# A four-layer graph network on one core: rows spread over the partitions by transfers, the projection a round ahead, a new order of steps

## What is computed

```
x = layernorm(x + L0(x, adj))    # s1, s2 = Wh @ a1, Wh @ a2
                                 # att = softmax(leaky_relu(s1[i] + s2[j]), masked by adj);  att @ Wh
x = layernorm(x + L1(x, adj))    # softmax of leaky_relu(bilinear logits), elu(x W1 + att x W2)
x = layernorm(x + L2(x, adj))    # 4-head attention, softmax over j; relu(heads @ Wo + bo)
x = layernorm(x + L3(x, adj))    # relational convolution; adj is 0 or 1, so one relation is live
```

## Time and profile before

| | |
|---|---|
| time, median of 3 runs | 496.18 us (496.12 to 496.77) |
| profiled execution | 496.9 us |
| its span, first to last instruction | 495.0 us |
| busy TensorE / ScalarE / VectorE / GpSimd | 468.4 / 428.0 / 410.8 / 370.6 us |
| mean granted TensorE clock | 0.988 |

### The profile page before, as it was taken

The page is one execution under the profiler, slowest core; times in us unless marked ns, Lnnn a source line. Parts: engine busy times, 40 slices in busy tenths (PEclk is TensorE's granted clock), DMA queues, the critical chain, the costliest instruction groups (busy, mean ns, idle before and its releaser), DMA issues. The chain is left out here.

```text
span 495.0 us, 13988 instructions
## 1 busy us (share of the span) xinstructions
PE 468.4 (95%) x3872; PEld 402.3 (81%) x3872; DVE 410.8 (83%) x1605; ACT 428.0 (86%) x1261; POOL 370.6 (75%) x736
## 2 busy tenths in 40 slices
PE   6968999999999999999999999999999999999793
PEld 5756778988888888988888888888888888877572
DVE  5657898998888998898888988898898989876653
ACT  3558999999999999999999999999999999988750
POOL 1365576788888888888888888888888888986523
PEclk9989999999999999999999999999999999999997
DMA  7211111122112221222112221221123100000011
...
DMA packets 40222, 26.93 MB, mean 54 GB/s; under 512 B 2641, under 2 KB 39889, under 8 KB 40146
## 3 DMA queue, kind: packets, MB, share of 16 engines
...
...
## 5 line engine op out<-in xcount | busy, mean ns | idle before, releaser
L1211 POOL TENSOR_SCALAR x<-y,minus_mean,rstd 128x128 f32<-128x128 f32 x244 | 144.8, 601 | 6.8 <-issue 5.1
L788 ACT ACTIVATE p<-p,nmax 128x256 f32<-128x256 f32 x256 | 128.5, 530 | 0.4 <-DVE nmax L981 0.4
L981 DVE CUSTOM_DVE_ANT_0 p<-ps,neg 128x256 f32<-128x256 f32 x256 | 90.7, 420 | 2.3 <-PE ps L564 2.3
L1193 POOL TENSOR_TENSOR rstd<-ve,minus_half 128x2 f32<-128x2 f32 x128 | 91.1, 712 | 0.0
L575 PE MATMUL ps<-ident,p 128*128 128x128 f32 x512 | 78.0, 275 | 4.1 <-DVE nmax L981 3.4
L1186 POOL TENSOR_SCALAR ve<-stats 128x2 f32<-128x2 f32 x128 | 24.6, 192 | 72.3 <-DVE stats L896 64.9
L797 ACT COPY p2T<-ps 128x512 f32<-128x512 f32 x128 | 75.2, 590 | 1.3 <-PE ps L575 0.5
L575 PEld LDWEIGHTS ps<-ident,p 128*128 128x128 f32 x512 | 61.3, 143 | 9.3 <-DVE nmax L981 4.0
L788 ACT ACTIVATION_READ_ACCUMULATOR p<-p,nmax 128x1 f32 x256 | 56.1, 219 | 0.0
L896 DVE BATCH_NORM_STATS2 stats<-y 128x6 f32<-128x256 f32 x128 | 54.1, 423 | 1.5
L1175 POOL TENSOR_TENSOR relu<-relu,neg 128x512 f32<-128x512 f32 x32 | 37.1, 1161 | 21.1 <-ACT relu L757 21.1
(11 more groups left out here) (130 smaller groups left out, 1210.3 us busy)
## 6 DMA issues: line engine op xcount, KB each, us to landing
...
```

The source lines that it names most:

```text
L788: last = nc.scalar.activation(p2(n)[:, k, a, :], p2(n)[:, k, a, :], ACT.Exp, bias=nmax2(n)[:, k, a:a + 1], scale=-1.0, accum_out=sum2(n)[: ...
L981: last = nc.vector.tensor_tensor_reduce(p2(n)[:, k, a, :], bank("sc2", n, a)[:, k * N:(k + 1) * N], neg2(n)[:, k, :], -1.0, HIGHEST, ALU.a ...
L1193: nc.gpsimd.tensor_tensor(rstd[layer](n), ve[layer](n), minus_half[:, :], ALU.pow)\
L1211: last = nc.gpsimd.tensor_scalar(dst[:, k, 0:D], y_t[layer](n)[:, k, :], minus_mean[layer](n)[:, k:k + 1], rstd[layer](n)[:, k:k + 1], ALU ...
```

## The change

**s2 by transfer.** From graph 3 on, s2_rows and c_s2 do not run. The projection gets a column more (131), so that xw0 has s2 and 0.2 s2 side by side. s2_out stores these two columns to DRAM (256 pieces of 8 bytes), s2_in loads them back as one row of 512 numbers into all 128 partitions (256 KB), the two values of a node next to each other. e0 then takes both inputs from SBUF, each at every second word. xw0 gets 4 buffers for 3, s2row 3 for 2.

**Reciprocal rows by transfer.** rs_rep is gone. rs_rows transposes the 128 x 8 reciprocals once, c_rs copies 8 x 128 to rs_turned, and rs_in spreads each of the 8 rows over 32 partitions by two transfers from SBUF to SBUF. onT2 waits for these.

**Signals.** The two signals of a layer's variance and mean become one counted twice.

**Order.** All places are new. The projection runs one round earlier against sc2, pT0 one round earlier, hg3 one round later, store one round later; the three flag steps stand at the end; the weights are loaded ahead of the second xT and the first adj.

```
-    "sync": [("ld_xT", 6707), ("ld_adj", 7906), ("ld_w", 8043), ("ld_x", 8602), ("aside", 16291), ("store", 19013)],
+    "sync": [("ld_xT", 7696), ("ld_w", 7941), ("s2_out", 8199), ("s2_in", 9000), ("ld_adj", 9574), ("ld_x", 10290),
+        ("rs_in", 14953), ("aside", 16550), ("store", 20067)],
...
+PE_ROWS = 3
...
+    **{step: (0, PE_ROWS) for step in ("s2_rows", "c_s2")},
+    **{step: (PE_ROWS, 0) for step in ("s2_out", "s2_in")},
...
+            def rs_in(n):
+                sp.wait_ge(sem("rs_sb"), n + 1)
+                free(sp, "rs_row", n, "onT_sb")
+                for k in range(T):
+                    sp.dma_start(rs_row(n)[:, k * P:(k + 1) * P],
+                                 rs_turned(n)[k * HEADS:(k + 1) * HEADS].rearrange("h (a i) -> h a i", a=1)
+                                 .broadcast_to((HEADS, DK, P))).then_inc(sem(f"rs_in{n % RING['rs_row']}"), 16)
+
+            def s2_out(n):
+                sp.wait_ge(sem("wh_sb"), n + 1)
+                sp.dma_start(s2_dram[n].rearrange("(t p) c -> p t c", p=P), xw0(n)[:, :, 1:3])\
+                    .then_inc(sem(f"s2_out{n % 2}"), 16)
+
+            def s2_in(n):
+                sp.wait_ge(sem(f"s2_out{n % 2}"), 16 * ((n - PE_ROWS) // 2) + 16)
+                free(sp, "s2row", n, "e0_ready")
+                sp.dma_start(s2row(n).rearrange("p j c -> p (j c)"),
+                             s2_dram[n].rearrange("(a j) c -> a (j c)", a=1).broadcast_to((P, 2 * N)))\
+                    .then_inc(sem(f"s2_in{n % RING['s2row']}"), 16)
...
             def rs_rows(n):
...
-                pe.wait_ge(sem("rs_rep_ready"), n + 1)
-                for k in range(T):
-                    last = pe.transpose(o[:, k * P:(k + 1) * P], rs_rep(n)[:, k, :], ident[:, :])
-                last.then_inc(sem("rs_ps"), 1)
+                pe.wait_ge(sem("rsum2_ready"), n + 1)
+                pe.transpose(o[0:T * HEADS, 0:P], rsum2(n).rearrange("p t h -> p (t h)"), ident[:, :])\
+                    .then_inc(sem("rs_ps"), 1)
...
             def e0(n):
-                dve.wait_ge(sem("s2_sb"), n + 1)
+                if n < PE_ROWS:
+                    dve.wait_ge(sem("s2_sb"), n + 1)
+                    row = bank("s2_rows", n)[:, 0:N]
+                else:
+                    dve.wait_ge(sem(f"s2_in{n % RING['s2row']}"), 16 * ((n - PE_ROWS) // RING["s2row"]) + 16)
+                    row = s2row(n)[:, :, 0]
                 free(dve, "p0", n, "pT_ps0")
                 for k in range(T):
...
+                    last = nc.vector.scalar_tensor_tensor(out=p0(n)[:, k, :], in0=row, scalar=xw0(n)[:, k, 0:1],
+                                                          in1=s2row(n)[:, :, 1], op0=ALU.add, op1=ALU.max)
...
-            def rs_rep_(n):
-                pool.wait_ge(sem("rsum2_ready"), n + 1)
-                free(pool, "rs_row", n, "rs_ps")
-                nc.gpsimd.tensor_copy(rs_rep(n).rearrange("p t (h d) -> p (t h) d", h=HEADS),
```

More of the change, by code:

```diff
@@ L191, in build @@
         eq1 = ring("eq1", [T, N])
-        xw0_all = sb("xw0", [P, RING["xw0"], T, D + 3])
+        xw0_all = sb("xw0", [P, RING["xw0"], T, D + 4])
         xw0 = lambda n: xw0_all[:, n % RING["xw0"]]
-        s2row = ring("s2row", [N])
+        s2row = ring("s2row", [N, 2])
         p0 = ring("p0", [T, N])
@@ L239, in build @@
         rsum2 = ring("rsum2", [T, HEADS])
-        rs_rep = ring("rs_rep", [T, D], of="rs_row")
+        rs_turned = ring("rs_turned", [P], of="rs_row")
         ps = ctx.enter_context(nc.psum_tensor("ps", [P, 8, 512], F32))
@@ L254, in build @@
         x3_dram = nc.dram_tensor("x3_aside", (B, P, T * D), F32, kind="Internal").ap()
+        s2_dram = nc.dram_tensor("s2_rows", (B, N, 2), F32, kind="Internal").ap()
         x_v = t["x"].rearrange("b (t p) d -> b p t d", p=P)
@@ L355, in _ @@
             sp.dma_start(first_w[:, :], t["first_w"]).then_inc(sem("w0_loaded"), 16)
-            run("sync", {"ld_adj": ld_adj, "ld_xT": ld_xT, "ld_x": ld_x, "ld_w": ld_w, "aside": aside, "store": store})
+            run("sync", {"ld_adj": ld_adj, "ld_xT": ld_xT, "ld_x": ld_x, "ld_w": ld_w, "rs_in": rs_in, "s2_out": s2_out, "s2_in": s2_in, "aside": aside, "store": store})
             for s in range(RING["x4"]):
@@ L389, in setup @@
                 pe.wait_ge(sem("w0_loaded"), 16)
-                pe.matmul(ps[:, 0, 0:2], first_w[:, W0], first_w[:, 0:2], start=True, stop=True)\
+                pe.matmul(ps[:, 0, 0:3], first_w[:, W0], first_w[:, 0:3], start=True, stop=True)\
                     .then_inc(sem("setup_pe"), 1)
@@ L434, in flag @@
                 pe.wait_ge(sem("excess_ready"), 2)
-                pe.matmul(o[0:1, 0:1], excess[:, :], xw0_all[:, 0, 0, D + 2:D + 3], start=True, stop=True)\
+                pe.matmul(o[0:1, 0:1], excess[:, :], xw0_all[:, 0, 0, D + 3:D + 4], start=True, stop=True)\
                     .then_inc(sem("excess_ps"), 1)
@@ L473, in proj0 @@
                 for k in range(T):
-                    last = pe.matmul(o[:, k * (D + 2):(k + 1) * (D + 2)], xT0(n)[:, k * P:(k + 1) * P], w0_w[:, :],
+                    last = pe.matmul(o[:, k * (D + 3):(k + 1) * (D + 3)], xT0(n)[:, k * P:(k + 1) * P], w0_w[:, :],
                                      start=True, stop=True)
@@ L712, in c_proj0 @@
                 free(act, "xw0", n, "agg_ps0")
-                nc.scalar.copy(xw0(n)[:, :, 0:D + 2],
-                               bank("proj0", n)[:, 0:T * (D + 2)].rearrange("p (t d) -> p t d", t=T))\
+                nc.scalar.copy(xw0(n)[:, :, 0:D + 3],
+                               bank("proj0", n)[:, 0:T * (D + 3)].rearrange("p (t d) -> p t d", t=T))\
                     .then_inc(sem("wh_sb"), 1)
@@ L719, in c_s2 @@
                 free(act, "s2row", n, "e0_ready")
-                nc.scalar.mul(s2row(n), bank("s2_rows", n)[:, 0:N], SLOPE).then_inc(sem("s2_sb"), 1)
+                nc.scalar.mul(s2row(n)[:, :, 1], bank("s2_rows", n)[:, 0:N], SLOPE).then_inc(sem("s2_sb"), 1)
             def c_rs(n):
                 act.wait_ge(sem("rs_ps"), n + 1)
-                free(act, "rs_row", n, "onT_sb")
-                nc.scalar.copy(rs_row(n), bank("rs_rows", n)[:, 0:N]).then_inc(sem("rs_sb"), 1)
+                if n >= RING["rs_row"]:
+                    act.wait_ge(sem(f"rs_in{n % RING['rs_row']}"), 16 * T * (n // RING["rs_row"]))
+                rows = slice(0, T * HEADS)
+                nc.scalar.copy(rs_turned(n)[rows, :], bank("rs_rows", n)[rows, 0:P]).then_inc(sem("rs_sb"), 1)
             def exp0(n):
@@ L899, in e0 @@
             def e0(n):
-                dve.wait_ge(sem("s2_sb"), n + 1)
+                if n < PE_ROWS:
[4 more added lines that the diff above has]
+                    row = s2row(n)[:, :, 0]
                 free(dve, "p0", n, "pT_ps0")
                 for k in range(T):
-                    last = nc.vector.scalar_tensor_tensor(out=p0(n)[:, k, :], in0=bank("s2_rows", n)[:, 0:N],
-                                                              scalar=xw0(n)[:, k, 0:1], in1=s2row(n),
-                                                              op0=ALU.add, op1=ALU.max)
+                    last = nc.vector.scalar_tensor_tensor(out=p0(n)[:, k, :], in0=row, scalar=xw0(n)[:, k, 0:1],
+                                                          in1=s2row(n)[:, :, 1], op0=ALU.add, op1=ALU.max)
                 last.then_inc(sem("e0_ready"), 1)
@@ L988, in r2 @@
                 dve.wait_ge(sem("p_ready2b"), n + 1)
-                free(dve, "rsum2", n, "rs_rep_ready")
+                free(dve, "rsum2", n, "rs_ps")
                 nc.vector.reciprocal(rsum2(n), sum2(n)).then_inc(sem("rsum2_ready"), 1)
@@ L993, in onT2 @@
                 dve.wait_ge(sem("agg_ps2"), n * HEADS + HEADS)
-                dve.wait_ge(sem("rs_sb"), n + 1)
+                dve.wait_ge(sem(f"rs_in{n % RING['rs_row']}"), 16 * T * (n // RING["rs_row"] + 1))
                 free(dve, "onT", n, "wo_ps")
@@ L1226, in _ @@
             run("gpsimd", {
-                "neg2": neg2_, "rmask1": rmask1, "rs_rep": rs_rep_,
+                "neg2": neg2_, "rmask1": rmask1,
                 "var0": lambda n: variance(0, n), "rsq0": lambda n: rsqrt(0, n), "norm0": lambda n: norm(0, n),
@@ L1252, in packed @@
         "xT": turned("x"),
-        "first_w": _np.concatenate([_np.reshape(i["L0_gnn_a"], (2, width)).T, turned("L0_gnn_W"), i["L0_gnn_W"]], 1),
+        "first_w": _np.concatenate([_np.reshape(i["L0_gnn_a"], (2, width)).T[:, [0, 1, 1]], turned("L0_gnn_W"),
+                                    i["L0_gnn_W"]], 1),
         "l1_w": _np.concatenate([i["L1_gnn_W"], turned("L1_gnn_a_12"), i["L1_gnn_W_1"], i["L1_gnn_W_2"],
```

27 lines of the change are left out of this document (13 added, 14 removed), and 36 rows, old and new, of tables (PLAN, RING).

## The result

The changed kernel takes 581.66 us (579.34 to 583.99), the kernel before 496.48 us beside it: ratio 1.171, interval 1.165 to 1.177. The prediction, 489.0 us with a range of 484.2 to 496.0, was wrong by 93 us and on the wrong side.

A forecast was written before the change was run, and what follows sets the result against it. TensorE was taken as the bound, practically without a gap in 26 rounds of 13.95 us. Terms -5.5 - 0.2 - 0.3 - 1.7 + 0 + 0.5 = -7.2 us took 496.9 to 489.7, 489.0 on the median's scale; range 484.2 to 496.0.

The forecast's parts named there:

- What hangs on the transfers: SP's queue: rs_in and s2_in would land in time for onT2 and e0, e0 covered by 0.4 us at worst.
- Rival 4: s2_in lands late and e0 holds the round; at 6 us after issue some 18 us lost, 507 us; 3%.
- A TensorE instruction taken from the middle pays in full.: Middle 26 rounds: TensorE busy 362.45 of 362.76 us, so removed work there shortens the time by its full length.
- s2 rows, -5.5: TensorE: dropping the two s2_rows transposes saves 0.22 us in each of 25 dense rounds, -5.5 us.
- Reciprocal rows, -0.3: TensorE: one 8-column transpose with two shape changes replaces two transposes, saving 0.01 us a round, -0.3 us.
- Rival 1: TensorE: the 8-column operand of rs_rows costs no entry; 2.6 us more go, 484.4 to 486.4 us; 20%.
- Order, -1.7: TensorE: a projection, a pT0 and an hg3 move out of the dense rounds into fill and drain, -1.7 us.
- rival 3: VectorE: e0 doubles through stride and lock, VectorE becomes the bound at 14.26 us a round, 503 us; 6%.
- Bank waits: TensorE: z1 takes the PSUM bank freed by y0, with a lead of about 0.5 us, so no wait.
- Fill, 0: Start: later loads of xT(1) and adj(0) against earlier steps filling TensorE's idle time; 0, ends -2 and +1.5 us.
- drain, +0.5: End: graph 31's reciprocal rows by transfer, landing in 2 to 3 us, cost +0.5 us, ends 0 and +2.

The follow-up runs named there:

- e_order2: Changed kernel with s2 and reciprocal rows both back on TensorE, new order kept, c_rs put behind c_v2 and e0 a little later; 513.2 us.
- b_s2: Kernel before, in its own order, with only the s2 transfers and, for them, xT load, projection and its copy one round ahead; 502.6 us.
- e_mix2: As e_mix, with s2_out moved behind the xT load in SP's round; 492.72 us, ratio 0.992 to the kernel before.
- e_e1: As e_rs_pe2, with eq1 and masks moved behind y2b on VectorE; 500.0 us.
- e_actq_e1: As e_rs_actq, with eq1 and masks moved behind y2b on VectorE; 503.5 us.
- e_rs_pe2: Changed kernel with reciprocal rows back on TensorE and c_rs put behind c_v2, s2 transfers and new order kept; 502.9 us.
- e_mix: As e_actq_e1, with the last three graphs' reciprocal rows made on TensorE; 496.8 us, ratio 1.000 to the kernel before.
- e_rs_actq: Changed kernel with the two rs_in transfers issued from ScalarE's queue instead of SP's; 511.8 us.

## Why the prediction was wrong, step by step

- **What hangs on the transfers: the step that failed.** It priced rs_in and s2_in, each alone, with issues of 0.34 to 0.47 us and the landing times of a queue that was mostly empty. It listed SP's new order and didn't ask which of its waits ends last: rs_in's does, 245.8 us of SP's waiting in all, so the other transfers of the round stopped being spread over it. The adjacency load, moved to a place behind six of them, was not priced at all, and it was the longest wait, 45.5 us at masks. Issues were 2.2 to 2.3 us for the two behind rs_in; landings 5.3 to 6.6 us. Rival 4 had the kind of mechanism (a transfer too late, "from about 5 us after issue on"), at 3%, and named only s2_in; e0 does wait for it, 29.3 us. Its price was also too low by its own figures: issued at 3.5 us and landing at 6, s2_in is there at 9.5, against 8.2 for e0 and 0.2 to 0.4 of room in VectorE, so 0.9 to 1.1 us a round late, not 0.7. The loop back to rs_in through c_rs was not seen, and it makes the delay lasting: each round is as long as the loop, 16.4 us as a rule.
- **"A TensorE instruction taken from the middle pays in full."** The reading of the earlier trace rows was too strong. TensorE's busy time covers short waits: in e_order2 the window of a round (209.12 to 223.53) has it busy 14.37 of 14.41 us, and the rows above, from that round, show its weights waiting 0.44 us for e1, by which the transposes are 0.2 us late. In b_s2 0.22 us less work gave nothing. The chain z1, relu, masked relu, e1, bank had little slack in the kernel before: e1's last piece ended about 0.3 us ahead of hg3 (243.31 and two pieces of 0.42 in the earlier trace rows, 244.44 in the earlier trace rows).
- **s2 rows, -5.5.** The size was right where nothing else takes its place: e_mix2's usual round is 0.28 us shorter than before, and these two transposes are gone from it (0.22). That they give all of it is argued from the rows; in b_s2, the one run with this part alone, they gave nothing.
- **Reciprocal rows, -0.3.** Mis-sized: e_e1 to e_actq_e1 differ by this part alone and by 3.4 us in the middle. In e_mix2, start to start, the projection takes 228.88 - 228.43 = 0.45 and rs_rows 229.08 - 228.88 = 0.20:

```profile
228.43 0.61 PE L498 MATMUL ps<-first_w,xT 128*128 128x131 f32 x4
228.88 0.27 PE L522 MATMUL ps<-ident,rsum 128*8 128x128 f32 x1
229.08 1.15 PE L593 MATMUL ps<-qkT 32*128 32x256 f32 x16
```

  Together 0.65, against 0.54 + 0.22 before: 0.11 a round, 2.9 us in 26. The 8-column operand has no entry of its own, and the 0.10 ahead of sc2 moved from the projection to rs_rows. Rival 1 was right in substance, though the figure named for it (0.11 to 0.15 behind rs_rows, with 0.54 ahead) had the entry in the wrong place.
- **Order, -1.7.** Not borne out. In the change it put masks and eq1 ahead of e1 and beside GpSimd's masked relu, worth 0.17 to 0.25 us a round (e_e1, e_actq_e1), and z1 directly behind agg2, where it takes 0.97 us (e_rs_pe2) instead of 0.87, while the transpose that stood there before loses 0.05. The shift of steps into fill and drain was not measured by itself.
- **e0 and rival 3.** In the changed kernel e0 didn't double (551 ns on average): its place keeps it mostly away from the masked relu. In b_s2 it did, 875 ns. The Trainium skill's rule that the prediction weighed (SBUF — State Buffer, "SBUF: two separate sides"), that such instructions lock each other out whole, agrees with b_s2: there the masked relu takes 1.44 us and the second piece ends 0.28 us behind its end. What decides is which instruction stands beside which; y1b's and y2b's means in the earlier trace rows said nothing of that.
- **Bank waits.** z1 did not wait for y0, as forecast. The bank that mattered was z1's own, held until e1 has read it; the working looked only at the bank that the removed step had used.
- **Fill, 0, and drain, +0.5.** Measured +10.8 up to sc2 of graph 2, and +8.2. In the drain the row's transfer takes what was put at 2 to 3 us (chain of waits, then VectorE):

```profile
553.54 6.50 DMA rs_row<-rs_turned
...
560.12 0.42 DVE L1029 TENSOR_TENSOR onT<-ps,rs_row 128x256 f32<-128x256 f32 x1 [3.07 <-DMA rs_row<-rs_turned]
```

  e_mix, without that transfer in the last three graphs, has a drain of 31.0 us. In the fill the first s2_out held up the loads behind it; e_mix2 moved it, and sc2 of graph 2 came 3.5 us sooner than in e_mix. Moving rs_in to ScalarE's queue had brought 6.1 before (68.8 in e_rs_actq, 74.9 in the changed kernel).

The sum, -7.2 us, looks close to what e_mix2 gains in the middle, 6.3 us (356.49 against 362.76). That is in part luck: the reciprocal rows gave about 2.6 us more than their term, and of the order's 1.7 nothing could be shown. It also needed four repairs first.
